# Two layers of attention and a routed FFN on one core: four engine lists from a list scheduler in place of one shared step list

## The reference

```python
x = x + global_latent_attn(rmsnorm(x, norm1_w), ...)   # causal softmax(q k^T) v
x = x + local_gqa_attn(rmsnorm(x, norm2_w), ...)       # keys of the last 32 positions
...
sw1, sw2 = (_bit_quant(shared_w1), _bit_quant(shared_w2))
shared_out = silu(h @ sw1.T) @ sw2.T
top_idx = argmax(softmax(h @ router_w.T))
routed_out = gate * expert[top_idx](h)
x = x + _layernorm(shared_out + routed_out)
```

## Time and profile before

| what | value |
|---|---|
| median of 3 runs | 899.52 us (895.91 to 899.82) |
| the profiled execution | 890.55 us, its span 888.8 us |
| granted clock, mean | 0.801 |
| busy in the span | PE 513.0, DVE 367.3, ACT 359.0, POOL 193.6 us |

### The profile page before, as it was taken

The page is one execution under the profiler, slowest core; times in us unless marked ns, Lnnn a source line. Parts: engine busy times, 40 slices in busy tenths (PEclk is TensorE's granted clock), DMA queues, the critical chain, the costliest instruction groups (busy, mean ns, idle before and its releaser), DMA issues.

```text
span 888.8 us, 16219 instructions
## 1 busy us (share of the span) xinstructions
PE 513.0 (58%) x6400; PEld 274.2 (31%) x6400; DVE 367.3 (41%) x1010; ACT 359.0 (40%) x490; POOL 193.6 (22%) x480
## 2 busy tenths in 40 slices
PE   2146767756866756666666666625546436436463
PEld 1033434433333333232322232213423213213331
DVE  3755462450250150013001300056666666676666
ACT  0127446537756736775677577602101001001100
POOL 3475471341260160013001300021010110110000
PEclk9978777979779969896989799856687677677667
DMA  6000000000000000000000000000000000000000
GB/s 187 1 1 2 1 2 1 2 2 1 1 2 2 1 1 1 1 2 1 2 1 1 1 1 1 1 1 2 1 6 1 6 7 0 7 6 1 6 7 6
DMA packets 8809, 6.22 MB, mean 7 GB/s; under 512 B 1816, under 2 KB 8096, under 8 KB 8736
## 3 DMA queue, kind: packets, MB, share of 16 engines
q10 hardware_dynamic: 3424, 2.68, 1.1%
q1 hardware_dynamic: 5312, 2.52, 1.1%
HBM read 4.15 MB, written 1.05 MB: 6 GB/s over the span
## 4 chain that ended last, share of the span: by engine, by line
DVE 26%; PE 25%; issue 19%; ACT 17%; POOL 12%; DVEq 0%; SPq 0%; DMA 0%; POOLq 0%; ACTq 0%
ACT prob L749 16%; PE scores L901 6%; PE osum_g L927 5%; PE misc L1024 3%; PE scores L896 3%; PE misc L1035 2%; DVE early L1379 2%; DVE early L1418 2%; DVE early L1408 1%; DVE early L1421 1%; PE misc L868 1%; POOL ke_g L680 1%; PE misc L927 1%; PE misc L879 1%; POOL ny_g L653 1%
## 5 line engine op out<-in xcount | busy, mean ns | idle before, releaser
L749 ACT ACTIVATE prob<-scores 128x1024 f32<-128x1024 f32 (+3 forms) x352 | 306.7, 923 | 191.5 <-PE scores L901 191.3
L927 PE MATMUL osum_g<-prob,V 128*32 128x256 f32 (+1 forms) x2304 | 177.8, 435 | 38.8 <-ACT prob L749 32.4
L901 PE MATMUL scores<-qT,kT 32*128 32x256 f16 (+3 forms) x1520 | 72.6, 272 | 91.4 <-ACT prob L749 81.7
L927 PEld LDWEIGHTS osum_g<-prob,V 128*32 128x32 f32 x2304 | 70.9, 123 | 111.8 <-issue 92.9
L689 POOL TENSOR_SCALAR_AFFINE_SELECT prob<-prob 128x512 f32<-128x512 f32 x64 | 41.9, 666 | 256.9 <-ACT prob L749 255.8
L901 PEld LDWEIGHTS scores<-qT,kT 32*128 32x128 f16 x1520 | 25.2, 94 | 153.0 <-issue 143.2
L1288 DVE RECIPROCAL rec_g<-misc 128x16 f32<-128x16 f32 x16 | 4.1, 257 | 129.8 <-PE misc L944 127.5
L1035 PE MATMUL misc<-t2T,h1p 128*128 128x512 f16 x128 | 38.5, 454 | 31.2 <-DVE h1p L1411 31.2
L1288 DVE RECIPROCAL rec_l<-misc 128x16 f32<-128x16 f32 x16 | 4.1, 257 | 114.6 <-PE misc L944 112.2
L706 POOL TENSOR_SCALAR frs<-fmv 128x1 f32<-128x1 f32 x16 | 3.1, 191 | 205.8 <-DVE fmv L1434 205.8
L1024 PE MATMUL misc<-early,t1T 128*128 128x256 f16 x256 | 41.6, 340 | 3.6 <-DVEq L1382 3.6
(11 more groups left out here) (228 smaller groups left out, 807.3 us busy)
## 6 DMA issues: line engine op xcount, KB each, us to landing
X<-in_L_attn_hidden_dram SPq DMA_DIRECT2D x8, 128.0 KB, 4.8
early<-in_L_ffn_expert_w_dram ACTq DMA_DIRECT2D x1, 1024.0 KB, 7.5
out_dram<-X SPq DMA_DIRECT2D x16, 64.0 KB, 1.5
rope<-in_rope_dram SPq DMA_DIRECT2D x1, 256.0 KB, 3.4
early<-in_L_ffn_shared_w_dram ACTq DMA_DIRECT2D x2, 128.0 KB, 9.1
band<-in_band_dram ACTq DMA_DIRECT2D x1, 80.0 KB, 3.1
wraw_l<-in_L_attn_l_wq_dram ACTq DMA_DIRECT2D x1, 64.0 KB, 2.4
ident<-in_ident_dram SPq DMA_DIRECT2D x1, 64.0 KB, 2.3
```

Source lines behind the costliest of these rows:

```text
L749: act.activation(prob[:, n % NP, 2 * half:2 * half + 2, lo:hi], src, ACT.Exp, scale=float(HD) ** -0.5 * QSCALE ** -2).then_inc(exp_done, 1)
L901: ins = pe.matmul(scores[:, 512 * m + c:512 * m + c + w], kT[a][rows, g, P * (t % kept[a]):P * (t % kept[a]) + P], qT[a][rows, b % Q_KEPT[ ...
L927: ins = pe.matmul(o[32 * m:32 * m + 32, q:q + w], V[a][:, t % kept[a], g, :], prob[:, n % NP, m, c:c + w], start=(first and k == 0), stop= ...
```

## The change

The shared list is gone. `Steps` writes down every engine's part of every step as an operation of its own, with a duration, the operations it needs, and the bank of `misc` it takes and until when (some 120 lines, one `op` call for each operation). `levels` gives each operation the length of the longest chain behind it, `urgency` scales that by two numbers for each class (KNOBS), and `make_plan` runs four engines in step: on each it takes the most urgent operation that is ready. The result is a list for each engine (ORDER) and the order of units; an engine's parts can stand in another order than another engine's. Both score halves can be planned apart, but with "whole" at 99.0 all units but one stay whole.

In the program itself three things differ. The three Newton steps stand together in POOL's `proj`. `bound` is two steps. The score product signals twice, behind the last matmul of each half of its heads, and each exponential waits for its own half's signal; the product still waits for both exponentials of the unit before.

```diff
-COST = {
-    "split": [(DVE, 1.7)], "ksplit": [(POOL, 1.9)], "newton": [(POOL, 1.9)],
...
-HOP = 0.803
-PULL = {
-    "pv": -0.5, "close": 0.806, "local": 0.9, "attend": 0.169, "norms": 0.447, "feed": 0.0, "front": 0.5, "qk": 0.0,
...
+HOP = (0.22, 0.1, 0.08, 0.2)
+KNOBS = {
+    "half1": 106.2,
+    "half0": -9.0,
+    "whole": 99.0,
...
+    "norms": (1064.741, 249.0),
...
+    "feed": (0.927, -16.0),
...
+        op((POOL, "proj", a, b), 4.55, (DVE, "proj", a, b), *old(DVE, "split", a, p), *old(POOL, "ksplit", a, p))
+        op((POOL, "ksplit", a, b), 2.66, (POOL, "proj", a, b), *old(PE, "kT", a, p))
...
+        best = None
+        for e in range(4):
+            if options[e]:
+                t = max(free[e], min(o[0] for o in options[e]))
+                o = max((o for o in options[e] if o[0] <= t + knobs["look"]), key=lambda o: o[1])
+                t = max(free[e], o[0])
+                if best is None or t < best[0]:
+                    best = (t, e, o[2])
...
-            def exp(*u):
+            def exp(a, b, g, pr, half):
+                u = (a, b, g, pr)
                 n = UNIT[u]
-                a, b, g, pr = u
-                act.wait_ge(qk_done, n + 1)
+                act.wait_ge(qk_done, 2 * n + half + 1)
...
                 if n:
-                    pe.wait_ge(exp_done, 2 * n)
+                    pe.wait_ge(exp_done, 2 * n - (half == 0))
...
-                ins.then_inc(qk_done, 1)
+                        if k == len(ps) - 1 and m in (1, GRP - 1):
+                            ins.then_inc(qk_done, 1)
...
-            for kind, *at in PLAN:
-                if kind in run:
-                    run[kind](*at)
+            for kind, *at in ORDER[PE]:
+                run[kind](*at)
```

More of the change, by code:

```diff
@@ L80, in local_scores @@
[L80 to L98, removed]
@@ L101, in weight_steps @@
[L101 to L105, removed]
-PE, DVE, POOL, ACT_E = range(4)
-COST = {
[L111 to L121, removed]
-}
@@ L146 @@
[L146 to L166, removed]
@@ new lines, in followers, with levels @@
+def followers(steps):
+    out = defaultdict(list)
+    for k, needs in steps.need.items():
+        for n in needs:
+            out[n].append(k)
+    return out
+def levels(steps):
+    after = followers(steps)
+    scores = [("E", G, b, *u) for b in range(NB) for u in units_of(G, b)]
+    for x, y in zip(scores, scores[1:]):
+        after[x].append(y)
+    level = {}
+    for root in steps.ops:
+        stack = [] if root in level else [(root, iter(after[root]))]
+        while stack:
+            k, rest = stack[-1]
+            n = next((n for n in rest if n not in level), None)
+            if n is not None:
+                stack.append((n, iter(after[n])))
+                continue
+            stack.pop()
+            e, t = steps.ops[k]
+            level[k] = t + max([level[n] + HOP[e] * (steps.ops[n][0] != e) for n in after[k]], default=0.0)
+    return level
@@ new lines, with urgency @@
+CLASS = {"prep": "weights", "bound": "weights", "ternary": "weights", "wturn": "weights", "scales": "weights",
+         "stat": "front", "norm": "front", "xT": "front", "proj": "front", "ksplit": "front", "split": "front", "kT": "front",
+         "qT": "front", "pv": "pv", "oevac": "oevac", "oT": "close", "onT": "close", "wo": "close", "fstat": "norms", "fxa": "norms",
+         "fh": "norms"}
+def urgency(steps, knobs):
+    out = {}
+    for k, v in levels(steps).items():
+        name = "unit" + "gl"[k[1]] if k[0] in ("Q", "E", "M") else CLASS.get(k[1], "feed")
+        if name in ("front", "close", "pv"):
+            name += "gl"[k[2]]
+        by, plus = knobs.get(name, (1.0, 0.0))
+        out[k] = v * by + plus
+    return out
@@ new lines, with __init__, run @@
+class Clock:
+    def __init__(self, start=0.0):
+        self.start, self.work, self.rate = start, 0.0, 1.0
+    def run(self, t, d):
+        while True:
+            while t >= self.start + CLOCK_WINDOW:
+                share = self.work / CLOCK_WINDOW
+                if self.rate == 1.0 and share < CLOCK_DROP:
+                    self.rate = 0.5
+                elif self.rate < 1.0 and share >= CLOCK_RISE:
+                    self.rate = 1.0
+                self.start, self.work = self.start + CLOCK_WINDOW, 0.0
+            room = self.start + CLOCK_WINDOW - t
+            if d <= room * self.rate:
+                self.work += d / self.rate
+                return t + d / self.rate
+            self.work += room
+            t, d = t + room, d - room * self.rate
@@ new lines @@
+STEPS = Steps()
+ORDER, TAKE, UNIT_LIST, _ = make_plan(STEPS, urgency(STEPS, KNOBS), KNOBS)
+TAKE.update({("weights", j): (j, 0) for j in range(NMISC)})
+def number():
+    unit = {u: n for n, u in enumerate(UNIT_LIST)}
+    pv, osum, ends = {}, {}, {}
+    for s in [s for s in ORDER[PE] if s[0] == "pv"]:
+        pv[s[1:]] = len(pv)
+        if s[1] == G and s[2:4] not in osum:
+            osum[s[2:4]] = len(osum)
+        ends.setdefault(s[1:4], [s[1:], s[1:]])[1] = s[1:]
+    masks = {s[1:]: n for n, s in enumerate([s for s in ORDER[POOL] if s[0] == "qk"])}
+    return unit, pv, osum, masks, ends
@@ L789, in _ @@
                    "fw1s": fw1s, "fact": fact}
-            for kind, *at in PLAN:
-                if kind in run:
-                    run[kind](*at)
+            for kind, *at in ORDER[ACT_E]:
+                run[kind](*at)
         @block.tensor
@@ L1445, in _ @@
                    "fh1": fh1, "fsel": fsel, "fsum": fsum, "fout": fout}
-            for kind, *at in PLAN:
-                if kind in run:
-                    run[kind](*at)
+            for kind, *at in ORDER[DVE]:
+                run[kind](*at)
 def tables():
```

501 lines of the change are left out of this document (276 added, 225 removed).

## The result

The changed kernel takes 582.88 us in the median of 4 runs (581.88 to 583.79), against 897.71 us (890.90 to 899.82) for the kernel before beside it: a ratio of 0.650, 95% interval 0.646 to 0.654. The profiled execution took 583.79 us, its span is 582.0 us. The forecast was 624 us with a range from 588 to 695: the direction and most of the mechanism hold, but the time lies 41 us under the forecast and 5 us under the range.

The account below looks back on a forecast made before the run. Score products and exponentials waiting for each other were taken to pace the attention, with the FFN a separate chain behind it. Start 36 + attention 469 - 8 + 30 + block 7's 51 + 38 = 616 us span, 624 us measured; range 588 to 695.

Parts of the forecast that it names:

- What bounds the kernel: In the attention, score products and exponentials wait for each other at one `scores` tile; this loop takes 417 us over 171 slots.
- The overflow: In the attention, whole PE steps overfill 74 of 171 slots, most with an `fw1` or `fw2`, by 52 us in all.
- Stalls: In the attention, PE standing at steps not ready, FFN steps included, costs 30 us, between bounds of 0 and 88.
- the 88 us of before: In the earlier kernel's attention, the part of 117 us lost that was put down to PE standing at fronts not ready.
- Rival A: In the attention, stalls stay as they were, 88 us: 674 us of span, 683 us measured; chance 0.27.
- The half signal: In the attention, the first exponential starts 0.1 us earlier in about 97 slots: 8 us gained, bounds 0 and 15.
- The clock: In the attention, a fuller PE keeps the higher clock, over 0.85 granted, so full-clock rows were used.
- Rival C: In the attention, PE is granted the lower clock; slots add up to about 676 us, 833 us measured; chance 0.03.
- The start and the tail: First score product at about 36 us (35 to 39); from the last global unit to the end about 89 us.
- The median: For the whole kernel, the median of runs is 1.010 of the profiled execution, which gave 624 us.
- The rule against it: In the attention, the FFN's DVE steps get longer beside POOL's steps: about 10 us of DVE time over 98 steps.
- Rival B: In the attention, steps fit nearly without loss, stalls 5 us: 583 us of span, 591 us measured; chance 0.14.

## Why the prediction was wrong in size

Three rows of the changed kernel's timeline cut its span into the parts of the sum: the first score product, the last global exponentials, the last residual step.

```profile
34.83 0.51 PE L953 MATMUL scores<-qT,kT 32*128 32x256 f16 x8 [3.11 <-DVEq L1338]
...
490.66 2.88 ACT L801 ACTIVATE prob<-scores 128x1024 f32<-128x1024 f32 x3
...
541.43 0.42 DVE L1361 TENSOR_TENSOR X<-misc,X 128x256 f32<-128x256 f32 x1 [1.29 <-PE misc L1016]
```

The start is 34.8 us (36 forecast), the attention from there to 493.54 us 458.7 (469 - 8 + 30 = 491), block 7's local layer to 541.85 us 48.3 (51), block 7's FFN to 582.0 us 40.2 (38). That is 34 us less span than the forecast of 616, and 32 of them are in the attention: the steps that failed are the two terms in it that stand for lost time, the overflow first, then the stalls.

- **What bounds the kernel**: right. The loop of 417 us, read from two undisturbed slots of before, is the floor of the changed kernel too; its undisturbed slots are 2.51 us.
- **The overflow, 52 us, is the step that failed.** It had two faults. The slots were filled with lengths of bars where PE works from start to start: the earlier trace rows show it already, where `pv` starts 0.33 us behind a product of 0.40. And `fw1` was taken at 2.43 us, from a stretch granted 0.71, while I argued in the same breath that the attention would be granted more; it takes 1.85. So a slot with an `fw1` overflows by 0.66 us, not 1.4; and only 22 of 171 held an `fw1` or `fw2`, so these can't be most of 74. The prediction had 422 us of PE work in the 171 slots; PE is occupied 380 us in them. With its idle gaps taken off, its steps overrun the loop by 32 us and not 52: 16 in slots with an `fw1` or `fw2`, 6 in the one stalled slot of block 1. Half of the products of `fw1` and `fw2` left out give back some 10 us, and 25 of the 29 fronts and closings with no FFN lose 14 us, stalls included, where I had counted 29 us of overfill alone for all of them. By the trace all slots with FFN steps lose 17 us. The right lengths were open to me: the new table has 0.33, 1.0 and 2.0 us for a score product, a `pv` and an `fw1`, and the plan drawn from it ends, by its own reckoning, at 587 us, where the span was 582.
- **Stalls, 30 us**: too long as well. The slots with front, closing or weights steps lose 21 us, overfill included, 9 of them in the one stall of block 1. The check on the 88 us of before was misread too: of the 162.6 us in the earlier trace rows, 20.4 are the wait before the first exponential, outside the attention, so that some 60 and not 80 us are PE standing at steps of a front. The reason given for a value near none was right and understated: with FFN and weights where they were, the stalls of before are already gone. Rival A needed late steps; one shared order (83 us) and wrong durations (179 us) each bring them, so own lists and read durations both bear on this term, as far as one shared order and one wrong table can show it.
- **The half signal, 8 us**: 3.8 measured.
- **The clock**: over 0.85 forecast, 0.98 granted. Rival C falls; the full-clock rows were right, but not used for `fw1`.
- **The start and the tail**: right within 3 us each; the last global unit ends 88.5 us ahead of the end (89 forecast).
- **The median**: taken as 1.010 of the profiled execution, as before; here it is 0.998, which made the forecast 7 us too long. How one kernel's profiled run stands to its median does not carry over to the next.
- **The rule against it**: DVE's busy time rose from 367.3 to 377.8 us, which looks like the 10 us estimated for the FFN's steps; but with the durations summed by step, only 5.7 us of the rise are the FFN's, and 3.0 are `ternary`, so the match is in part luck. The Trainium skill, "SBUF — State Buffer", section "SBUF: two separate sides", says that a DVE step with two SBUF inputs and a GpSimd step that reads SBUF shut each other out at a shared pair of ports; this trace agrees in kind (line 1206 of `ternary`, 4.18 us beside POOL's mask and 2.19 later). But PE waited for DVE and POOL together only 17.5 us in the stretch, and the cost lies beside other work.

Rival B (591 us) came nearest. Its title, steps fit nearly without loss, holds in the main, but its number is in part luck: it kept the overflow at 52 us, which was 32, and cut the stalls to 5 and raised the half signal to 12, which was 3.8.

The range's upper end adds up to 692 us by its own terms, not 695; nothing hangs on it.

The Trainium skill, in "Perfetto Trace Analysis", section "Optimization Strategy", says that where the most-contended engine changes over time, interleaving those regimes may help. The experiment with the FFN behind the attention agrees: the FFN under the attention is worth 159 us here, and costs the attention 16.

## What to carry to other kernels

Fill slots by the starts of consecutive steps at the clock that the new place will have, not by the lengths of bars from a stretch with another clock. A static order is worth as much as its durations: read them from a trace, ask the plan for its own end, give each engine a list of its own, and look for a short step that stands behind an engine's long wait. Where two stages have different engines in front, put one under the other; what it costs is read slot by slot.

## What the runs showed of the hardware

For a full unit, four matmuls for two heads kept PE 0.32 us from start to start and eight for four heads 0.33 (bars of 0.39 and 0.40), both in stretches granted 0.98. So a score product in two halves that stand apart keeps PE 0.64 us, almost twice as long, and the matmuls of the four heads ran side by side. And for the same matmuls PE was busy 513.0 us before and 439.9 after, at 0.801 and 0.938 granted in the mean: in the attention PE was busy 66% at 0.85 before and 83% at 0.98 after, and its work itself got shorter.
